# Attention scores in pairs of heads: QK matmuls ordered by head instead of by key tile

## The chip, the cores and the metric

One Trainium2 chip, all 8 cores, the same program on each with its own input. Cores 2b and 2b+1 share batch element b of four; each computes 2048 of its 4096 rows and holds all 4096 for keys and values. The metric is the device time of the slowest core in microseconds (us). TensorE is PE in the profile, VectorE DVE, ScalarE ACT, GpSimd POOL.

## The reference

Layernorm, attention with 16 heads of 64, residual; then layernorm, a mixture of 8 experts with a shared expert, residual. The change lies in the attention alone:

```python
Q = circulant(x, wq_c, wq_b)      # K, V the same; circulant = a dense 1024x1024 product
attn_logits = jnp.einsum('bqhd,bkhd->bhqk', Q, K) * scale   # scale = 64 ** -0.5
attn_weights = jax.nn.softmax(attn_logits, axis=-1)
out_heads = jnp.einsum('bhqk,bkhd->bqhd', attn_weights, V)
out = circulant(out_merge, wo_c, wo_b)
```

## The kernel before

Every instruction goes through `Sched.op`, which appends it to a list of its engine; line 77 issues them later, in that order, so all rows of the profile carry L77 and groups are told apart by tiles. An engine's instructions are issued in the order of its list, and an instruction with `waits` holds up what stands behind it until the named semaphores have reached their counts.

The stages are: layernorm and transposes of 4096 rows (to about 230 us); attention (to about 2330 us); output projection, second layernorm, router; the feed-forward part in 20 units; the output.

Attention runs over 8 pairs of heads (`p`, line 386). The two heads of a pair lie on the two halves of the partitions: head 0 on rows 0 to 63 of `QTp` and `KTp`, head 1 on rows 64 to 127. Each pair has 4 chunks of 512 queries (`c`, line 422), and each chunk 16 groups of two key tiles of 128 (`gi`, line 424). A group does, in the order in which it is written down:

- four QK matmuls (lines 437 to 448), 64 rows deep, 128 keys x 512 queries each: two key tiles for each of the two heads, into `psS[0]` for head 0 and `psS[1]` for head 1 (two banks each). The first matmul of head 0 waits until the exp of the group before has read `psS[0]` (`wsa`), the first of head 1 the same for `psS[1]` (`wsb`). The last matmul of each head counts up `pQK`.
- four PV matmuls of the group before (`emit_pv`, line 403), two for each head, into `psO`; each pair waits for the exp that made its weights.
- two exps on ACT (lines 452 to 461), one for each head, 128 x 1024 from `psS` into one of three buffers of `PT`. The exp of head 0 waits for `pQK` at one less than its count after the group's last QK. Unit u = 2 x group + head also waits for the PV matmuls of unit u - 3, which read the same buffer of `PT`.
- projection jobs of the next pair (`ProjQ.drain_to`, line 465): 4 for q, 8 for k, 32 for v, in this order, dealt out evenly over the 64 groups; a q or k job is 8 matmuls of 128x512, a v job 8 of 128x128. The last pair has none.

At the end of a chunk the PVs of the last group are done, then the row sums are copied (`lscr`), spread by matmuls of ones into `psS[1]`, inverted on DVE (`invl`), multiplied in (`stg`), and the two heads are put together by two matmuls that work on rows 0 to 63 (`identB`, `shift64`), before the QKs of the next chunk.

These lines set what an exp waits for:

```python
ws = [("pQK", nqk_b - (1 if h == 0 else 0))]
if u >= 3:
    ws.append(("pPV", pv_at[u - 3]))
```

Of the kernel before, what the change touches and what calls it, by code (L numbers as in the profile page):

```python
# [83 lines left out]
def build_program(dbg=(), last_phase=6):  # L84
# [33 lines left out]
    with ExitStack() as ctx:  # L118
# [145 lines left out]
        with ExitStack() as c2:  # L264
# [121 lines left out]
            for p in range(NPAIR):  # L386
                bp = p % 2
                if p + 2 < NPAIR:
                    emit_wdma(p + 2)
                if p + 1 < NPAIR:  # L390
                    nq = ProjQ(p + 1, [("pQK", pair_end[p - 1]["pQK"]),
                                       ("pPV", pair_end[p - 1]["pPV"])]
                               if p > 0 else [])
                else:
                    nq = None

                exp_at = {}
                pv_at = {}
                recip_at = {}
                evac_at = {}  # L400
                pend = []

                def emit_pv(job):
                    u, cc_, pts, h = job
                    ws = [("aE", exp_at[u])]
                    if u % UPC <= 1:
                        ws.append(("vT", evac_at.get(cc_ - 1, S.n("vT"))
                                   if cc_ > 0 else S.n("vT")))
                    vsl = slice(65 * h, 65 * h + 65)
                    k0_, glen_ = groups[(u % UPC) // 2]  # L410
                    for i in range(glen_):
                        kt = k0_ + i
                        S.op("tensor", "matmul",
                             psO[0:65, 512 * h:512 * h + 512],
                             Vp[bp][:, kt, vsl],
                             PT[:, pts, i * 512:(i + 1) * 512],
                             start=(kt == 0), stop=(kt == 31),
                             waits=ws if i == 0 else (),
                             inc="pPV" if i == glen_ - 1 else None)
                    pv_at[u] = S.n("pPV")  # L420

                for c in range(NCH):
                    qsl = slice(c * 512, (c + 1) * 512)
                    for gi, (k0, glen) in enumerate(groups):
                        ua = c * UPC + 2 * gi
                        ub = ua + 1
                        wsa = []
                        wsb = []
                        if ua >= 2:
                            wsa.append(("aE", exp_at[ua - 2]))  # L430
                            wsb.append(("aE", exp_at[ub - 2]))
                        else:
                            wsa = [("vT", S.n("vT")), ("vP", proj_done[p])]
                            wsb = list(wsa)
                        if c > 0 and ua == c * UPC:
                            wsb.append(("vT", recip_at[c - 1]))
                        for i in range(glen):
                            kt = k0 + i
                            for h, slot, ws0 in ((0, 0, wsa), (1, 1, wsb)):
                                rowsl = slice(64 * h, 64 * (h + 1))  # L440
                                S.op("tensor", "matmul",
                                     psS[slot][:, i * 512:(i + 1) * 512],
                                     KTp[bp][rowsl, kt * 128:(kt + 1) * 128],
                                     QTp[bp][rowsl, qsl],
                                     start=True, stop=True,
                                     tile_position=(64 * h, 0),
                                     waits=ws0 if i == 0 else (),
                                     inc="pQK" if i == glen - 1 else None)
                        nqk_b = S.n("pQK")
                        while pend:  # L450
                            emit_pv(pend.pop(0))
                        for h, u in ((0, ua), (1, ub)):
# [3 lines that stand above are left out]
                            S.op("scalar", "activation",  # L456
                                 PT[:, u % 3, 0:glen * 512],
                                 psS[u % 2][:, 0:glen * 512],
                                 AF.Exp, bias=C_M12, scale=C_EIGHTH,
                                 waits=ws, inc="aE")  # L460
                            exp_at[u] = S.n("aE")
                        pend.append((ua, c, ua % 3, 0))
                        pend.append((ub, c, ub % 3, 1))
                        if nq is not None:
                            nq.drain_to((2 * gi + 2) / UPC / NCH + c / NCH)
                    while pend:
                        emit_pv(pend.pop(0))
                    S.op("vector", "tensor_copy", lscr[64:65, 0, :],
                         psO[64:65, 0:512],
                         waits=[("pPV", None), ("pT", None)], inc="vT")  # L470
                    S.op("vector", "tensor_copy", lscr[64:65, 1, :],
                         psO[64:65, 512:1024], inc="vT")
                    S.op("tensor", "matmul", psS[1][0:64, 0:512],
                         onescolF[64:65, 0:64], lscr[64:65, 0, :],
                         start=True, stop=True,
                         waits=[("vT", None), ("aE", None)], inc="pT")
                    S.op("tensor", "matmul", psS[1][0:64, 512:1024],
                         onescolF[64:65, 0:64], lscr[64:65, 1, :],
                         start=True, stop=True, inc="pT")
                    S.op("vector", "reciprocal",  # L480
                         invl[0:64, :, :].rearrange("p a b -> p (a b)"),
                         psS[1][0:64, 0:1024],
                         waits=[("pT", None)], inc="vT")
                    recip_at[c] = S.n("vT")
                    S.op("vector", "tensor_tensor", stg[0:64, 0, :],
                         psO[0:64, 0:512], invl[0:64, 0, :], ALU.mult,
                         waits=[("vT", None), ("pT", None)], inc="vT")
                    S.op("vector", "tensor_tensor", stg[0:64, 1, :],
                         psO[0:64, 512:1024], invl[0:64, 1, :], ALU.mult,
                         inc="vT")  # L490
                    S.op("tensor", "matmul", psO[:, 0:512], identB[0:64, 0:128],
                         stg[0:64, 0, :], start=True, stop=False,
                         waits=[("vT", None)])
                    S.op("tensor", "matmul", psO[:, 0:512], shift64[0:64, 0:128],
                         stg[0:64, 1, :], start=False, stop=True, inc="pT")
                    S.op("vector", "tensor_scalar", outT[:, p, qsl], psO[:, 0:512],
                         biasT[:, 2 * NDT + p:2 * NDT + p + 1], None, ALU.add,
                         waits=[("pT", None)], inc="vT")
                    evac_at[c] = S.n("vT")
                if nq is not None:  # L500
                    nq.finish()
                pair_end[p] = {"pQK": S.n("pQK"), "pPV": S.n("pPV"),
                               "vT": S.n("vT")}

                if p == 0:
                    if "qt" in dbga:
                        S.op("gpsimd", "dma_start", out=dbga["qt"], in_=QTp[0][:],
                             waits=[("vP", proj_done[0])], inc="dbg90", inck=16)
                    if "kt" in dbga:
                        S.op("gpsimd", "dma_start", out=dbga["kt"], in_=KTp[0][:],  # L510
                             waits=[("vP", proj_done[0])], inc="dbg91", inck=16)
                    if "vt" in dbga:
                        S.op("gpsimd", "dma_start", out=dbga["vt"],
                             in_=Vp[0][:].rearrange("p a b -> p (a b)"),
                             waits=[("vP", proj_done[0])], inc="dbg92", inck=16)
# [478 lines left out]
```

How the kernel before makes its waits and increments, by code:

```python
            def runner(e, lst=lst):  # L72
                for meth, args, kw, ws, ih in lst:
                    for h, v in ws:
                        if v > 0:
                            e.wait_ge(h, v)
                    ins = getattr(e, meth)(*args, **kw)
                    if ih is not None:
                        ins.then_inc(*ih)
```

## Time and profile before

| | us |
|---|---|
| two timed runs | 5250.03, 5609.47 (median 5429.75) |
| profiled execution | 5131.93 |
| its span, slowest core (core 2) | 5130.4 |
| spans of the 8 cores | 5106.4 to 5130.4 |
| PE busy, share of the span | 3955.7, 77% |
| DVE busy | 1627.0, 32% |
| ACT busy | 1535.2, 30% |

The profile is of one execution and shows its slowest core. A busy time is the union of an engine's instructions; the idle time of a group is what the engine stood still just before instructions of that group, put down to what ended it. PEclk is the share of TensorE's 2.4 GHz that was granted: 1.00 is 2.4 GHz, 0.50 is 1.2 GHz, and what lies between is a mix of the two over a stretch.

### The profile page before, as it was taken

The page shows a single profiled execution, that of the slowest core. Times are in us where ns is not written, and L with a number is a line of the kernel's source. Part 1 is how long each engine was busy: PE and PEld are TensorE (multiplying, and loading weights), DVE is VectorE, ACT ScalarE, POOL GpSimd, SP SyncE. Part 2 cuts the span into 40 slices and gives each one's busy share as a digit, 9 for nine tenths or more (in the row PEclk, how much of TensorE's full clock was granted, in tenths as well). Part 3 has the DMA queues.
Part 4 walks back from the last instruction along what each step waited for, and adds up shares of the span by engine and source line. Part 5 has one row for each costly group of instructions (what it writes and reads, how often), then busy time and mean ns, then how long its engine had stood idle before and what let it go on. Part 6 is the DMA issues. An engine that isn't in the chain of part 4 may idle for free.

```text
span 5130.4 us, 58302 instructions; the slowest of 8 cores (5106.4 to 5130.4 us)
## 1 busy us (share of the span) xinstructions
PE 3955.7 (77%) x18399; PEld 1656.2 (32%) x18656; DVE 1627.0 (32%) x2454; ACT 1535.2 (30%) x1630; POOL 86.8 (2%) x107
## 2 busy tenths in 40 slices
PE   1566666666767676774359999999999999999996
PEld 0322222222222222111224444444444443444443
DVE  4322222222222122112344333333333434333344
ACT  3155555555555555551201111111111010111110
POOL 0100000000000000000000000000000000000000
PEclk9988888888888888666679999999999999999997
DMA  6300000000000000002142121212121213132103
GB/s 218 64 1 7 1 7 1 7 1 7 1 7 1 1 1 1 0 1 82 60 74 38 32 38 31 38 31 38 32 38 31 38 31 48 22 62 39 31 5 132
DMA packets 100824, 165.79 MB, mean 32 GB/s; under 512 B 28080, under 2 KB 69056, under 8 KB 100544
## 3 DMA queue, kind: packets, MB, share of 16 engines
q0 software_dynamic: 83072, 94.93, 12.2%
q1 hardware_dynamic: 17472, 67.11, 3.8%
q8 instruction: 177, 2.90, 0.2%
q14 instruction: 103, 0.84, 0.1%
HBM read 240.17 MB, written 16.78 MB: 50 GB/s over the span
## 4 chain that ended last, share of the span: by engine, by line
PE 69%; DVE 10%; ACT 10%; issue 8%; DMA 2%; DVEq 0%; ACTq 0%; POOL 0%; SPq 0%; POOLq 0%
PE psGU L77 30%; PE psD L77 15%; PE psS L77 9%; ACT PT L77 9%; PE psO L77 8%; DVE invl L77 4%; PE psP L77 4%; PE psT L77 1%; PE psC L77 1%; DMA xst<-xf 1%; DVE lscr L77 1%; DVE stg L77 1%; DVE us_sb L77 1%; DMA co_sb<-co 1%; DVE xnst L77 1%
## 5 line engine op out<-in xcount | busy, mean ns | idle before, releaser
L77 ACT ACTIVATE PT<-psS,consts 128x1024 bf16<-128x1024 f32 x1024 | 1182.2, 1199 | 1065.7 <-PE psS L77 1058.9
L77 ACT ACTIVATE gs_sb<-psGU 128x512 bf16<-128x512 f32 x440 | 262.7, 597 | 2143.4 <-PE psGU L77 2071.8
L77 PE MATMUL psD<-prod,wdh 128*128 128x512 bf16 x3449 | 778.9, 380 | 81.5 <-DVE prod L77 76.4
L77 PE MATMUL psGU<-xn2T,wgh 128*128 128x512 bf16 x3450 | 837.2, 383 | 4.2 <-issue 0.7
L77 PE MATMUL psGU<-xn2T,wuh 128*128 128x512 bf16 x3449 | 829.4, 380 | 3.9 <-issue 0.2
L77 PE MATMUL psS<-QTp,KTp 64*128 64x512 bf16 x2048 | 513.4, 421 | 308.3 <-ACT PT L77 296.8
L77 PE MATMUL psO<-PT,Vp 128*65 128x512 bf16 x2048 | 589.3, 411 | 26.4 <-ACT PT L77 26.4
L77 DVE TENSOR_TENSOR yacc<-yacc,psD 128x512 f32<-128x512 f32 x608 | 418.4, 688 | 371.2 <-PE psD L77 363.7
L77 PEld LDWEIGHTS psD<-prod,wdh 128*128 128x128 bf16 x3520 | 321.7, 97 | 538.7 <-issue 242.6
L77 DVE TENSOR_TENSOR us_sb<-psGU,ce_sb 128x512 bf16<-128x512 f32 x352 | 243.6, 692 | 793.4 <-PE psGU L77 793.4
L77 PEld LDWEIGHTS psGU<-xn2T,wgh 128*128 128x128 bf16 x3520 | 346.2, 99 | 423.8 <-issue 15.7
L77 PEld LDWEIGHTS psGU<-xn2T,wuh 128*128 128x128 bf16 x3520 | 346.1, 98 | 420.8 <-issue 9.9
L77 DVE CAST Vp<-psP 128x128 bf16<-128x128 f32 x256 | 75.4, 294 | 859.7 <-PE psP L77 859.7
L77 PEld LDWEIGHTS psO<-PT,Vp 128*65 128x65 bf16 x2048 | 193.8, 116 | 398.8 <-issue 309.7
L77 PEld LDWEIGHTS psS<-QTp,KTp 64*128 64x128 bf16 x2048 | 107.0, 96 | 600.2 <-issue 580.6
L77 DVE RECIPROCAL invl<-psS 64x1024 f32<-64x1024 f32 x32 | 209.6, 6550 | 116.1 <-PE psS L77 116.1
L77 PE MATMUL psO<-stg,identB 64*128 64x512 bf16 x32 | 18.6, 580 | 264.2 <-DVE stg L77 264.2
L77 DVE TENSOR_TENSOR prod<-gs_sb,us_sb 128x512 bf16<-128x512 bf16 x440 | 187.3, 426 | 84.6 <-DVE us_sb L77 83.5
L77 PE MATMUL psP<-cvp,xnT 128*128 128x128 bf16 x2048 | 166.8, 229 | 1.4 <-DVE KTp L77 0.6
L77 PEld LDWEIGHTS psP<-cvp,xnT 128*128 128x128 bf16 x2048 | 142.9, 103 | 67.4 <-issue 22.7
L77 PE MATMUL psS<-lscr,onescolF 1*64 1x512 f32 x128 | 104.6, 963 | 55.7 <-DVE lscr L77 55.7
L77 DVE COPY lscr<-psO 1x512 f32<-1x512 f32 x64 | 41.4, 684 | 322.3 <-PE psO L77 322.3
(105 smaller groups left out, 1215.5 us busy)
## 6 DMA issues: line engine op xcount, KB each, us to landing
xst<-xf SPq DMA_DIRECT2D x16, 2048.0 KB, 9.1
wgh<-wg POOLq DMA_DIRECT2D x8, 1536.0 KB, 15.0
wuh<-wu POOLq DMA_DIRECT2D x8, 1536.0 KB, 23.6
wdh<-wd POOLq DMA_DIRECT2D x8, 1536.0 KB, 30.2
wgh<-wg POOLq DMA_DIRECT2D x8, 1280.0 KB, 13.0
wuh<-wu POOLq DMA_DIRECT2D x8, 1280.0 KB, 19.4
wdh<-wd POOLq DMA_DIRECT2D x8, 1280.0 KB, 24.8
xo<-xf SPq DMA_DIRECT2D x4, 2048.0 KB, 10.8
```

The lines of the kernel that those rows point to most:

```text
L77: ins = getattr(e, meth)(*args, **kw)
```

## The change

The two loops around the QK matmul change places. Before, they are issued as head 0 tile 0, head 1 tile 0, head 0 tile 1, head 1 tile 1. After, both tiles of head 0 are issued and then both of head 1. Waits, counters, operands and everything else stay as they are.

```diff
-                        for i in range(glen):
-                            kt = k0 + i
-                            for h, slot, ws0 in ((0, 0, wsa), (1, 1, wsb)):
-                                rowsl = slice(64 * h, 64 * (h + 1))
+                        for h, slot, ws0 in ((0, 0, wsa), (1, 1, wsb)):
+                            rowsl = slice(64 * h, 64 * (h + 1))
+                            for i in range(glen):
+                                kt = k0 + i
                                 S.op("tensor", "matmul",
                                      psS[slot][:, i * 512:(i + 1) * 512],
                                      KTp[bp][rowsl, kt * 128:(kt + 1) * 128],
```

## Rows read from the trace of the kernel before

**Rows 1.** The page, first part: busy us (share of span) xinstructions.

```profile
span 5130.4 us, 58302 instructions; the slowest of 8 cores (5106.4 to 5130.4 us)
PE 3955.7 (77%) x18399; PEld 1656.2 (32%) x18656; DVE 1627.0 (32%) x2454; ACT 1535.2 (30%) x1630; POOL 86.8 (2%) x107
```

**Rows 2.** Windows: attention, and all behind it. Columns as the second line says.

```profile
core 2: us, PE busy (x) PEld busy (x) DVE busy (x) ACT busy (x) POOL busy (x), PEclk, DMA share, GB/s
228.00:2330.00 2102.00, 1446.51 (x6786) 525.65 (x6818) 443.64 (x507) 1182.20 (x1024) 15.79 (x18) 0.83 0.03 3
2330.00:5130.00 2800.00, 2442.01 (x11078) 1085.22 (x11298) 1085.09 (x1814) 314.27 (x539) 53.77 (x63) 0.94 0.24 44
```

**Rows 3.** Page, instruction groups: busy, mean ns | idle before, by releaser; last, waits.

```profile
L77 ACT ACTIVATE PT<-psS,consts 128x1024 bf16<-128x1024 f32 x1024 | 1182.2, 1199 | 1065.7 <-PE psS L77 1058.9
L77 PE MATMUL psS<-QTp,KTp 64*128 64x512 bf16 x2048 | 513.4, 421 | 308.3 <-ACT PT L77 296.8
...
PE psS L77 <- ACT PT L77: 296.8, 500, 1.5
```

**Rows 4.** Timeline, warm groups: start, duration, engine, xcount, idle before; last: narrow windows.

```profile
1092.65 2.30 ACT L77 ACTIVATE PT<-psS,consts 128x1024 bf16<-128x1024 f32 x2 [0.69 <-PE psS L77]
1093.29 0.65 PEld L77 LDWEIGHTS psP<-cvp,xnT 128*128 128x128 bf16 x8
1093.51 0.61 PE L77 MATMUL psP<-cvp,xnT 128*128 128x128 bf16 x8
1094.05 0.39 PE L77 MATMUL psS<-QTp,KTp 64*128 64x512 bf16 x1
...
1095.09 0.59 PE L77 MATMUL psS<-QTp,KTp 64*128 64x512 bf16 x3 [0.65 <-ACT PT L77]
...
1095.63 2.30 ACT L77 ACTIVATE PT<-psS,consts 128x1024 bf16<-128x1024 f32 x2 [0.69 <-PE psS L77]
...
1096.98 0.37 PE L77 MATMUL psS<-QTp,KTp 64*128 64x512 bf16 x1 [0.32 <-ACT PT L77]
...
1098.08 0.59 PE L77 MATMUL psS<-QTp,KTp 64*128 64x512 bf16 x3 [0.72 <-ACT PT L77]
...
1098.62 1.20 ACT L77 ACTIVATE PT<-psS,consts 128x1024 bf16<-128x1024 f32 x1 [0.69 <-PE psS L77]
...
1093.75 1.20 ACT L77 ACTIVATE PT<-psS,consts 128x1024 bf16<-128x1024 f32 x1
...
1095.30 0.37 PE L77 MATMUL psS<-QTp,KTp 64*128 64x512 bf16 x1
...
1095.61 1.05 PE L77 MATMUL psO<-PT,Vp 128*65 128x512 bf16 x4
...
1095.85 0.38 PE L77 MATMUL psO<-PT,Vp 128*65 128x512 bf16 x1
```

**Rows 5.** Timeline, groups with a k projection.

```profile
1053.33 0.61 PE L77 MATMUL psS<-QTp,KTp 64*128 64x512 bf16 x4
...
1053.87 1.05 PE L77 MATMUL psO<-PT,Vp 128*65 128x512 bf16 x4
...
1056.58 0.61 PE L77 MATMUL psS<-QTp,KTp 64*128 64x512 bf16 x4
```

**Rows 6.** Timeline, last pair, low clock; the last three from narrow windows.

```profile
2141.76 2.54 ACT L77 ACTIVATE PT<-psS,consts 128x1024 bf16<-128x1024 f32 x2 [0.91 <-PE psS L77]
...
2141.94 1.91 PE L77 MATMUL psO<-PT,Vp 128*65 128x512 bf16 x4
...
2145.21 2.54 ACT L77 ACTIVATE PT<-psS,consts 128x1024 bf16<-128x1024 f32 x2 [0.91 <-PE psS L77]
...
2141.38 0.63 PE L77 MATMUL psS<-QTp,KTp 64*128 64x512 bf16 x1
...
2142.37 0.63 PE L77 MATMUL psO<-PT,Vp 128*65 128x512 bf16 x1
...
2143.10 1.20 ACT L77 ACTIVATE PT<-psS,consts 128x1024 bf16<-128x1024 f32 x1
```

**Rows 7.** Windows by chunk, columns as in rows 2: first exp to start of the last.

```profile
1017.90:1068.10 50.20, 44.50 (x205) 16.41 (x208) 8.26 (x11) 35.56 (x31) 0.00 (x0) 0.97 0.00 1
1085.70:1132.60 46.90, 35.76 (x207) 14.87 (x206) 3.69 (x11) 35.55 (x31) 0.00 (x0) 0.97 0.00 1
1149.90:1197.40 47.50, 35.92 (x208) 15.15 (x206) 3.24 (x11) 35.66 (x31) 0.00 (x0) 0.93 0.00 1
2064.90:2111.60 46.70, 31.41 (x121) 8.99 (x120) 0.00 (x0) 35.72 (x32) 0.00 (x0) 0.93 0.00 1
2128.20:2181.00 52.80, 50.14 (x119) 11.79 (x120) 0.00 (x0) 37.19 (x31) 0.00 (x0) 0.50 0.00 0
2199.50:2248.20 48.70, 37.84 (x120) 9.97 (x120) 0.00 (x0) 36.23 (x32) 0.00 (x0) 0.77 0.00 0
2264.90:2317.80 52.90, 50.23 (x119) 11.79 (x120) 0.00 (x0) 37.12 (x32) 0.00 (x0) 0.50 0.00 0
...
301.50:348.00 46.50, 35.33 (x207) 14.82 (x206) 3.70 (x11) 35.57 (x32) 0.00 (x0) 0.98 0.00 1
```

**Rows 8.** Timeline, the start of a chunk.

```profile
1148.23 0.58 PE L77 MATMUL psS<-QTp,KTp 64*128 64x512 bf16 x1
1148.26 0.63 PE L77 MATMUL psO<-stg,shift 64*128 64x512 bf16 x1
```

## The prediction

> **What bounds the kernel now.** I read the page first, then stretches of the span, then single groups in the timeline. The page says that PE is busy 77% of the span and ACT 30% [rows 1]. Two stretches make up the span: attention, 2102 us, in which every QK, exp and PV of the kernel lies, and all that comes after it, 2800 us [rows 2]. The change touches only the first. The instruction groups show what is odd there: ACT works 1182 us on exps and stands idle 1066 us ahead of them, nearly all of it for the QK products in psS, while PE in turn waits 297 us for exps before it can write psS [rows 3]. Each waits for the other, so neither its busy time sets the pace; a loop does.
>
> The timeline of three key groups shows the loop [rows 4]. I call the two QK matmuls of head 0 A0 and A1, those of head 1 B0 and B1. From one first exp to the next it is 1095.63 - 1092.65 = 2.98 us, then 1098.62 - 1095.63 = 2.99, once with a v projection in it and once without. A0 goes out alone (1094.05, 1096.98), as soon as its half of psS is free. Then PE stands still 0.65 to 0.72 us, until expB has ended; then the other three QKs run, and 0.54 us after they began expA starts. So A1, which needs nothing from head 1, sits in PE's queue behind B0, which waits for expB. ACT pays for it: idle 0.69 us in each group. The period is 1.10 (expA to expB, 1092.65 to 1093.75) + 1.34 (expB to B0, 1093.75 to 1095.09) + 0.54 (B0 to expA) = 2.98.
>
> This holds for the groups with v projections and for those with none. With a q or k projection (8 matmuls of 512 columns) PE itself is full: the four QKs come out in one train of 0.61 us, and QK to QK takes 1056.58 - 1053.33 = 3.25 us [rows 5]. At the lower granted clock a group without projection takes 2145.21 - 2141.76 = 3.45 us [rows 6].
>
> How many of each: a pair of heads has 4 chunks of 16 groups. The jobs are dealt out evenly, so q and k fill chunk 0 and v the other three, for seven pairs; the eighth has none. A chunk from first expA to the start of the last expB takes 46.5 to 47.5 us in the v chunks (I looked at five), 50.2 in a q/k chunk, and 46.7 to 52.9 in the last pair, whose clock is 0.93, 0.50, 0.77, 0.50 [rows 7]. 46.9 - 1.1 = 45.8 is one slow interval of 4.0 and 14 of 2.99; 47.5 - 1.1 = 46.4 is two slow intervals of 3.4 and 3.8 and 13 of 2.99. So there are 7 x (14 + 13 + 13) = 280 warm groups of 2.99 us. In the last pair 196.7 us fit about 21 groups of 2.99 and 33 of 3.45.
>
> **The change, part by part.** No instruction is added or removed: 2048 QKs, as many weight loads, the same waits. Only B0 and A1 change places, and B0's wait now stands behind A1.
>
> *What goes.* A1 no longer waits for expB. In a warm group A0 starts at expA + 1.35 (1096.98 - 1095.63), A1 0.22 later, and its product is ready 0.53 us after it, at expA + 2.10. ACT is then still at expB (from 1.10 to 2.30). The old 0.69 us of idle goes.
>
> *What is late next.* Not ACT's own work. PT has three buffers, so expB of group g also waits for the first PV pair of group g-1 (pv_at[u - 3]). That pair stands in PE's queue behind B0 and B1 of group g, and B0 waits for expB of g-1. This closes a new loop, expB - B0 - B1 - PV - PV - expB. Its links from rows 4: expB to B0 1.34; B0 to B1 0.21 (1095.30); B1 to the first PV 0.31 (1095.61); to the second 0.24 (1095.85). The last link, second PV to expB, is not seen warm, since there it doesn't bind, but it is seen at the low clock: 2142.37 to 2143.10 = 0.73 us, and just there expB comes 1.34 us after expA instead of 1.10 [rows 6]: the wait is real. Two ways to carry it to the warm clock: the record is shorter by 0.63 - 0.38, giving 0.48; or the streaming of 512 columns is shorter (PV to PV 0.43 against 0.22), giving 0.52. I take 0.52. Sum: 1.34 + 0.21 + 0.31 + 0.24 + 0.52 = **2.62 us**, lower end 2.58. PE's own train has room in it: B0 to fourth PV 1.19, eight v matmuls and the step to A0 0.76 (1093.29 to 1094.05), A0 to A1 0.22, together 2.17. Saved per warm group: 2.99 - 2.62 = 0.37; 280 x 0.37 = **-104 us**.
>
> *Row halves.* The two heads use different halves of the array's rows. Four QKs take 0.61 us where four PVs take 1.05 [rows 5]: A and B run side by side. Queued as A0 A1 B0 B1, do they still? At a chunk's start, a QK matmul begins at 1148.23, ahead of the shift matmul at 1148.26 that stands before it in the queue [rows 8]. The shift works on rows 0 to 63, so that QK is B0 on rows 64 to 127, running ahead of A. The halves therefore keep their own order once nothing waits, and in the q/k groups I take the cost as 0. If B0 could only start together with A1, it would be one pass of 0.22 us more in 84 q/k groups (18 us) and 0.43 in 21 cold chunk starts (9 us); that is the bound from the other side. In the v and empty groups B0 has to wait for expB anyway, and the loss of concurrency costs only idle time of PE, already in the sum. The Trainium skill, "TensorE: Matmul & The Clock Gate", Part 3, has matmuls strictly first in, first out, which would give those 27 us and a sum of 5027. The order at 1148.23 disagrees, so the row decides.
>
> *At the low clock.* The same loop gives 1.34 + 0.43 + 0.56 (2141.38 to 2141.94) + 0.43 + 0.73 = 3.49 against 3.45. So the cold groups lose 0.04; with the cold starts of the v chunks +1 us.
>
> *The last pair.* It depends on the clock. If it stays cold as often as now: 21 x -0.37 + 33 x 0.04 = -6 us. If it warms up after three groups in each chunk: 4 x (3 x 3.49 + 12 x 2.62) = 168 against 196.7, -29 us. Now, cold, PE streams 7 passes of 0.43 in 3.45 us (87%) and the clock mostly stays low; cold v groups stream with no gap and reach the high level after two groups every time I looked (slow intervals of 3.4 and 3.8, then 2.99). After, A and B no longer share a pass: 8 x 0.43 in 3.49, 98%. That is nearer to the second case, so I take -29 and keep -6 for the range. "TensorE: Matmul & The Clock Gate", section "Why this matters for your kernels" in the Trainium skill, advises a continuously busy engine for the high level; it points the same way.
>
> *Chunk ends.* From the last expB to the next chunk's first expA nothing changes: two PVs, the sums, the 6.55 us reciprocal, the stg matmuls. The same projection jobs lie there. 0.
>
> **Sum.** The profiled execution took 5131.9 us for a span of 5130.4. 5131.9 - 104 + 1 - 29 = **5000 us**. The two runs shown before (5250.0 and 5609.5, median 5429.8) lie above it; the forecast is for an execution like the profiled one, and carries over as the ratio 0.974.
>
> **Rivals.**
> Main theory with the last pair's clock as now: 5131.9 - 104 + 1 - 6 = 5023, -2.1%.
> *ACT becomes the bound*: the PT wait doesn't bite when warm, and the next links decide: two exps of 1.10 give 2.21 us, 280 x 0.78 = 218 less, 4885. Against it stand the cold rows, in which the PT wait sets expB.
> *Weight loads come out of hiding*: two QKs in a row on the same rows can't load the second's weights during the first. Then B0 to B1 would be a whole matmul and load, 0.37 + 0.09 = 0.46 instead of 0.21, the loop 2.87, 280 x 0.12 = 34 less: 5098. Against it, B0 to B1 is already 0.21 with only A1 on the other rows between them.
> *Slower: the v chunks stay at the low clock.* Splitting the shared passes fills a cold v group: B0 to fourth PV 0.43 + 0.56 + 1.28, eight v matmuls at 0.11, the step 0.2, two QKs 0.86, about 4.1 us; with the empty ones at 3.5, 3.9 on average, 0.9 above now. All 280 cold would be +255, with -6 for the last pair 5381. Each cold group costs 0.9 and forfeits 0.37, so the sign turns at about 80 of 280. For it: the last pair does stay cold. Against it: PE has fewer gaps than now in every group.
> *Nothing happens*: expA keeps waiting for both heads. Its wait is the count reached with A1's increment, one short of B1's, before and after; little speaks for it.
>
> **Chances and range.** Main theory, last pair warm (5000): 0.45. Main, clock as now (5023): 0.25. Weight loads (5098): 0.10. Nothing (5132): 0.05. ACT bound (4885): 0.07. Low clock (over 5235): 0.08. The range takes the first three; downward it takes 2.58 as the loop's lower end (280 x 0.04 = 11 less) and a last pair that is warm from its first group (4 x 15 x 2.62 = 157, 11 less again), 4978, rounded to 4980; upward it ends at 5100. The 2% that a measurement can tell from no change is 103 us, below 5029. Faster: 0.45 + 0.07 + half of the 5023 case = 0.65. Within: the rest of it, 0.10 and 0.05 = 0.27. Slower: 0.08.
>
> **What would show it.** In v chunks, expA to expA 2.62 us, with expB 1.5 us after expA and released by PV; ACT's idle time ahead of the exps falls from 1066 to about 930 us, and part of it turns into waits for psO. A0 and A1 stand as two matmuls ahead of PE's wait, B0 and B1 behind. q/k groups stay at 3.25; 3.46 would mean that the halves don't run apart. v chunks take 41 to 42 us. I'd be wrong if the groups come out at 2.2 or 2.9, or if the v chunks show a clock well below 0.9.

## The result, and the profile after

The changed kernel takes 4994.9 us in the median of all its runs, the kernel before 5144.7 in the runs beside it. The ratio is 0.9722, with a 95% interval of 0.9682 to 0.9762: 2.8% faster. (In some executions of nearly every kernel here the cores of one die or both run at a lower clock for a part of the time; the ratios, and the times from here on, leave them out, and traces are read on cores that were not affected.) The forecast was 5000 us and a ratio of 0.974.

The profiled execution took 5029.6 us, with a span of 5028.1. It is 35 us above the median for one reason: behind attention this core and its neighbour, core 3, got a clock of 0.81 for about 250 us. Attention, where the change lies, is not touched by that on this core. Its page, first part, and the instruction groups that answer to [rows 3]:

```profile
span 5028.1 us, 58302 instructions; the slowest of 8 cores (4975.0 to 5028.1 us)
...
PE 4056.5 (81%) x18399; PEld 1677.0 (33%) x18656; DVE 1627.0 (32%) x2454; ACT 1541.6 (31%) x1630; POOL 86.8 (2%) x107
...
L77 ACT ACTIVATE PT<-psS,consts 128x1024 bf16<-128x1024 f32 x1024 | 1188.6, 1202 | 919.5 <-PE psS L77 846.1
...
L77 PE MATMUL psS<-QTp,KTp 64*128 64x512 bf16 x2048 | 601.3, 426 | 115.9 <-ACT PT L77 99.4
```

ACT does the same exps in nearly the same time and stands idle 920 us ahead of them instead of 1066. PE waits 99 us for exps instead of 297, and is busy longer with the same 2048 QKs (601 us against 513), because the two heads no longer share passes in most groups. Neither of the two busy times explains the gain.

Windows by chunk, as in [rows 7] (us, busy us of PE, PEld, DVE, ACT, POOL, PEclk, DMA share, GB/s): the q/k chunk and two v chunks of the fourth pair, the four of the last pair, then the 0.81 stretch:

```profile
959.60:1010.10 50.50, 45.60 (x205) 16.62 (x208) 8.26 (x11) 35.61 (x32) 0.00 (x0) 0.97 0.00 1
...
1027.40:1068.90 41.50, 38.47 (x207) 15.11 (x206) 3.69 (x11) 35.81 (x32) 0.00 (x0) 0.96 0.00 1
1084.70:1127.00 42.30, 39.15 (x208) 15.50 (x206) 3.24 (x11) 35.97 (x32) 0.00 (x0) 0.91 0.00 1
...
1929.00:1981.80 52.80, 51.50 (x120) 12.06 (x120) 0.00 (x0) 37.20 (x31) 0.00 (x0) 0.50 0.00 0
1998.40:2041.70 43.30, 37.00 (x120) 9.82 (x120) 0.00 (x0) 36.07 (x31) 0.00 (x0) 0.82 0.00 1
2057.90:2108.60 50.70, 48.28 (x120) 11.53 (x121) 0.00 (x0) 36.94 (x31) 0.00 (x0) 0.56 0.00 0
2125.50:2178.30 52.80, 51.40 (x119) 12.09 (x120) 0.00 (x0) 37.18 (x31) 0.00 (x0) 0.50 0.00 0
...
4710.00:4980.00 270.00, 252.76 (x963) 105.25 (x980) 93.99 (x148) 23.42 (x40) 0.57 (x1) 0.80 0.13 28
```

The same chunks took 50.2, 46.9 and 47.5 us. The last pair still spends most of its time at the low clock. I added up the trace of core 2 by kind of stretch. A chunk counts from the start of its first expB to that of its last, a chunk end from there to the next chunk's first expA:

| | before | after | difference | forecast |
|---|---|---|---|---|
| 21 v chunks | 963.6 | 854.6 | -109.0 | -103 |
| 7 q/k chunks | 345.6 | 345.7 | +0.1 | 0 |
| last pair | 196.6 | 195.3 | -1.3 | -29 |
| 31 chunk ends | 542.5 | 513.8 | -28.7 | 0 |
| behind attention | 2812.6 | 2849.7 | +37.1 (0.81 clock) | 0 |

The rest of the span changed by less than 1 us. On the cores of the other die, what lies behind attention takes 2808 to 2814 us, against 2805 to 2812 before. So the total came out right from four terms of which two were wrong, by amounts that nearly cancel: that part is luck.

The timeline of v groups in the changed kernel, and two narrow windows (the second PV, and B0 alone):

```profile
1045.61 2.30 ACT L77 ACTIVATE PT<-psS,consts 128x1024 bf16<-128x1024 f32 x2
...
1046.96 0.59 PE L77 MATMUL psS<-QTp,KTp 64*128 64x512 bf16 x2 [0.48 <-ACT PT L77]
...
1047.47 1.05 PE L77 MATMUL psO<-PT,Vp 128*65 128x512 bf16 x4
...
1048.19 1.20 ACT L77 ACTIVATE PT<-psS,consts 128x1024 bf16<-128x1024 f32 x1 [0.29 <-PE psO L77]
1048.36 0.61 PE L77 MATMUL psP<-cvp,xnT 128*128 128x128 bf16 x8
...
1049.66 2.32 ACT L77 ACTIVATE PT<-psS,consts 128x1024 bf16<-128x1024 f32 x2 [0.27 <-PE psS L77]
1050.06 1.05 PE L77 MATMUL psO<-PT,Vp 128*65 128x512 bf16 x4
...
1047.72 0.38 PE L77 MATMUL psO<-PT,Vp 128*65 128x512 bf16 x1
...
1049.54 0.37 PE L77 MATMUL psS<-QTp,KTp 64*128 64x512 bf16 x1
```

The exp at 1048.19 is an expB, and it waits for psO: the PV matmuls that free its PT buffer. The list of waits shows how often that happens, first before, then after (us in total, times, longest):

```profile
ACT PT L77 <- PE psO L77: 0.2, 1, 0.2
...
ACT PT L77 <- PE psO L77: 72.9, 207, 0.9
```

The new loop is there. From the B matmuls at 1046.96 to the next at 1049.54 it is 2.58 us, and PV to PV 1050.06 - 1047.47 = 2.59.

### The profile page after: what moved, and what is told of

Same layout as the page of the kernel before. It is cut to its first block, busy times and chain, and to the rows that moved or that the text cites. A ratio compares the mean times of both kernels' runs of the same rounds, so it can differ in the third digit from the quotient of the medians.

```text
span 5028.1 us, 58302 instructions; the slowest of 8 cores (4975.0 to 5028.1 us)
## 1 busy us (share of the span) xinstructions
PE 4056.5 (81%) x18399; PEld 1677.0 (33%) x18656; DVE 1627.0 (32%) x2454; ACT 1541.6 (31%) x1630; POOL 86.8 (2%) x107
## 4 chain that ended last, share of the span: by engine, by line
PE 76%; DVE 10%; ACT 6%; issue 5%; DMA 2%; DVEq 0%; ACTq 0%; POOL 0%; SPq 0%; POOLq 0%
PE psGU L77 31%; PE psD L77 15%; PE psS L77 11%; PE psO L77 10%; PE psP L77 6%; ACT PT L77 5%; DVE invl L77 4%; PE psT L77 1%; PE psC L77 1%; DMA xst<-xf 1%; DVE lscr L77 1%; DVE stg L77 1%; DVE us_sb L77 1%; DMA out<-obuf 1%; DVE xnst L77 1%
## 5 line engine op out<-in xcount | busy, mean ns | idle before, releaser
L77 PE MATMUL psD<-prod,wdh 128*128 128x512 bf16 x3449 | 791.6, 385 | 81.7 <-DVE prod L77 76.4
L77 PE MATMUL psGU<-xn2T,wgh 128*128 128x512 bf16 x3450 | 852.3, 388 | 4.5 <-issue 0.7
L77 PE MATMUL psGU<-xn2T,wuh 128*128 128x512 bf16 x3449 | 844.5, 386 | 4.1 <-issue 0.2
L77 PE MATMUL psS<-QTp,KTp 64*128 64x512 bf16 x2048 | 601.3, 426 | 115.9 <-ACT PT L77 99.4
L77 PE MATMUL psT<-identB,xnst 128*128 128x128 bf16 x256 | 32.3, 305 | 141.0 <-DVE xnst L77 141.0
```

Source lines behind the costliest of these rows:

```text
L77: ins = getattr(e, meth)(*args, **kw)
```

## Experiments

### Which loop sets the new period: a fourth PT buffer

```diff
-            PT = cc(nc.sbuf_tensor("PT", [128, 3, 1024], BF16))
+            PT = cc(nc.sbuf_tensor("PT", [128, 4, 1024], BF16))
...
-                            if u >= 3:
-                                ws.append(("pPV", pv_at[u - 3]))
+                            if u >= 4:
+                                ws.append(("pPV", pv_at[u - 4]))
```

(and u % 4 where u % 3 stood.) On the changed kernel:

> The changed kernel with four PT buffers instead of three, so that an exp waits for the PV matmuls of unit u - 4, which stand ahead of the B matmuls in PE's queue. Theory (after the change the loop expB - B0 - B1 - PV - PV - expB through the PT buffer sets the period of 2.59 us): it is broken, and the next one decides, from B0 over the four PVs to A0 and A1 of the next group, its two exps, and back to B0 after two groups: 1.50 + 0.22 + 0.54 + 1.10 + 1.34 = 4.70 us for two groups without a job, 0.45 more for each v job that it meets. v chunks at 2.45 to 2.55 a group on average, the sum over the 21 v chunks from 855 down to about 825 us, cold groups of the last pair from 3.45 to about 3.23; in all 30 to 40 us under the changed kernel's 4995, near 4960. Rival (the loop runs through psS, the buffer doesn't bind): v chunks stay at 855 us, 4995. Rival (ACT alone binds once PT is free): 2.21 a group, 4885.

It took 4936 us (one execution), against 4995. v chunks add up to 826 us. Core 4, the first chunk of the last pair, exps in sequence:

```profile
1930.11 4.49 ACT L77 ACTIVATE PT<-psS,consts 128x1024 bf16<-128x1024 f32 x4 [0.21 <-PE psS L77]
1934.81 4.49 ACT L77 ACTIVATE PT<-psS,consts 128x1024 bf16<-128x1024 f32 x4 [0.21 <-PE psS L77]
```

Two groups in 4.70 us, the sum named beforehand, and ACT idle 0.21 us in them. Neither rival survives: the buffer did bind, and ACT alone doesn't. In the v chunks the next loop lies close behind: from the fourth interval of each chunk on, 252 in all, a group takes 2.50 us on average instead of 2.59. The time fell by 59 us rather than 30 to 40, because the last pair also left the low clock (its chunk from 1914.4 to 1952.2, 37.8 us, ran at 0.92), which I had not counted on. Chunk ends grew again, to 525 to 530 us.

The same buffer on the kernel before:

> The kernel before with four PT buffers, nothing else. Theory: warm groups don't change (2.99 us), since there PV is done 0.35 us before expB could start; only groups at the low clock, where expB came 1.34 us after expA, gain 0.24 us each, some 33 in the last pair and 21 at chunk starts: -8 to -13 us, near 5122. Rival (the PT buffer already cost time before the change, and its wait was merely hidden by how the trace names releasers): v chunks fall by more than 20 us from 964.

5115.3 us in the median, ratio 0.9965 (0.9945 to 0.9984). v chunks stay at 965, so before the change the buffer cost nothing in a warm group. The gain lies in the last pair, core 2:

```profile
2054.00:2100.40 46.40, 31.84 (x121) 9.14 (x120) 0.00 (x0) 35.62 (x32) 0.00 (x0) 0.91 0.00 1
2116.20:2162.90 46.70, 31.36 (x120) 9.10 (x120) 0.00 (x0) 35.65 (x32) 0.00 (x0) 0.92 0.00 1
```

These are the first two chunks of the pair, which took 46.7 and 52.8 us before. In the second, 6 us is more than 0.24 us a group: the clock rose, here and in the last pair of all eight cores, with no matmul added. The sum over the pair fell by 15 us on core 2. The size is near the forecast of 8 to 13, but the way is partly another.

### Where the gain lies, and the row halves

```diff
-                        for i in range(glen):
+                        order = [(i, h) for h in (0, 1) for i in range(glen)]
+                        if c > 0 or p == NPAIR - 1:
+                            order = [(i, h) for i in range(glen) for h in (0, 1)]
+                        for i, h in order:
...
```

That is the new order in the q/k chunks alone; its counterpart has `if c == 0 and p < NPAIR - 1`, the new order everywhere else.

> The new order in chunk 0 of the seven pairs that carry q and k projections, the old order everywhere else. Theory (matmuls on different row halves keep their own order, so A0 A1 B0 B1 takes two passes like A0 B0 A1 B1 once nothing waits): the q/k chunks' sum stays at 345 us, the time within 3 us of 5132. Rival (strict order, three passes): 0.22 us more in 84 groups, q/k chunks at about 360 us, 5150.

> The counterpart of qk_chunks_only: the new order in the 21 v chunks and the last pair, the old one in the seven q/k chunks. Theory (the whole gain lies where B waits for its exp and PE has room): v chunks at 855 us, q/k chunks at 345, the time like the changed kernel's, 4995 within 8 us. Rival (part of the gain of the full change comes through the q/k chunks, by the clock with which the chunk behind them begins): above 5005.

The first gave 5130.8 us, ratio 0.9991 (0.9970 to 1.0012), with q/k chunks at 344 to 348 us. The second gave 4995.9, ratio 0.9742 (0.9714 to 0.9770), with v chunks at 854 to 855. So the q/k chunks cost nothing, and everything is gained in the rest. How A0 A1 B0 B1 costs no third pass can be seen in a q/k group of the changed kernel:

```profile
1004.93 0.61 PE L77 MATMUL psS<-QTp,KTp 64*128 64x512 bf16 x4
1005.47 1.05 PE L77 MATMUL psO<-PT,Vp 128*65 128x512 bf16 x4
...
1008.18 0.61 PE L77 MATMUL psS<-QTp,KTp 64*128 64x512 bf16 x4
```

The four QKs take 0.61 us as in [rows 5], and the group 3.25 us. Two narrow windows show that they start in pairs:

```profile
1004.93 0.39 PE L77 MATMUL psS<-QTp,KTp 64*128 64x512 bf16 x2
...
1005.16 0.38 PE L77 MATMUL psS<-QTp,KTp 64*128 64x512 bf16 x2
```

The trace doesn't name the heads. But A0 and A1 use the same rows, and two matmuls on the same rows, B0 and B1 in [rows 4], start 0.21 us apart. So the pair at 1004.93 is A0 and B0: B0 has overtaken A1.

### The last pair: is it the amount of work?

```diff
+                        if nq is None:
+                            for dt in range(NDT):
+                                S.op("tensor", "matmul", psP[gi % 2][:, 0:128],
+                                     xnT[:, dt, gi * 128:(gi + 1) * 128],
+                                     cvp[bp][:, dt, :],
...
```

> The changed kernel, and in every group of the last pair 8 more matmuls of 128x128 into a PSUM bank that nobody reads, where a v job would stand. Nothing of the result changes. Theory (the last pair stays at the low clock because it gives PE less work than the other pairs, whatever the order): its clock rises after two or three groups of each chunk, its groups go from 3.45 to 2.59 us, its chunks from 51.7 to about 42 us, together about 25 to 35 us less, near 4965, although PE does more. Rival (the clock in the last pair hangs on something else): the groups stay at the low clock and PE is full, 4.1 us each, 25 us or more above 4995.

4964.5 and 4968.8 us, ratio 0.9675 (0.9634 to 0.9717): 26 to 30 us under the changed kernel, by adding 512 matmuls that nobody needs. Its interval overlaps that of the changed kernel, but the traces tell the two apart: the last pair takes 163 us on all eight cores, against 190 to 201 without the filling. Core 2:

```profile
1928.50:1970.20 41.70, 40.38 (x241) 17.71 (x241) 0.00 (x0) 35.94 (x31) 0.00 (x0) 0.92 0.00 1
1986.10:2028.00 41.90, 40.29 (x240) 17.47 (x238) 0.00 (x0) 35.91 (x31) 0.00 (x0) 0.92 0.00 1
```

All four chunks of all eight cores do this, where on core 2 three of four ran at 0.50 to 0.56 without the filling. The runs with four PT buffers got there too, without added work but with shorter groups: 3.21 us against 3.45 at the start of a chunk in the old order.

### The chunk ends: order or clock?

Many chunk ends of the changed kernel are about 1.5 us shorter. The timeline of one in the kernel before, behind the first v chunk of the fourth pair:

```profile
1136.26 3.37 PE L77 MATMUL psS<-lscr,onescolF 1*64 1x512 f32 x4 [1.72 <-DVE lscr L77]
...
1139.73 6.55 DVE L77 RECIPROCAL invl<-psS 64x1024 f32<-64x1024 f32 x1 [3.72 <-PE psS L77]
```

And of the same one in the changed kernel:

```profile
1072.55 1.90 PE L77 MATMUL psS<-lscr,onescolF 1*64 1x512 f32 x4 [1.72 <-DVE lscr L77]
...
1074.55 6.55 DVE L77 RECIPROCAL invl<-psS 64x1024 f32<-64x1024 f32 x1 [2.25 <-PE psS L77]
```

The stall ahead is the same 1.72 us; the four fp32 matmul records (two matmuls in the program) take 3.37 us in the one and 1.90 in the other. Over all chunk ends of core 2 the time from their start to that of the reciprocal falls from 104.2 to 75.8 us, which is the whole gain of 28.7 to within 0.3. They took 2.34 to 3.64 us before; after, they take 1.90 behind 19 of the 21 v chunks, and still 2.08 to 3.64 behind the seven q/k chunks. The windows over just these stretches give the granted clock. Before, the stretch above and one of 3.64 us:

```profile
1136.20:1139.80 3.60, 3.37 (x4) 0.64 (x4) 0.07 (x1) 0.00 (x0) 0.00 (x0) 0.55 0.00 0
1071.70:1075.50 3.80, 3.64 (x4) 0.73 (x4) 0.00 (x0) 0.00 (x0) 0.00 (x0) 0.50 0.00 0
```

After:

```profile
1072.50:1074.60 2.10, 1.90 (x4) 0.45 (x4) 0.05 (x1) 0.00 (x0) 0.00 (x0) 1.00 0.00 0
```

To tell clock from order, the old order with six matmuls of no use in that stall:

```diff
+                    for m in range(6):
+                        S.op("tensor", "matmul", psP[nq.j % 2 if nq else 0][:],
+                             xnT[:, m % NDT, 0:128], xnT[:, m % NDT, 0:512],
...
```

> The kernel before, with only the 6 matmuls of 128x512 ahead of the matmuls of ones at every chunk's end. Theory (clock): the old order gets the short chunk ends too, 541 down to 515 or less over the 31 of them, near 5105. Rival (order): they stay at about 541, 5132.

5099.0 us, ratio 0.9917 (0.9890 to 0.9944); the 31 chunk ends fall from about 541 to 501.5 us, with v chunks at 961 to 963. A chunk end on core 7, with the filler ahead of it, and the granted clock over its fp32 matmuls:

```profile
1115.40 1.46 PE L77 MATMUL psP<-xnT 128*128 128x512 bf16 x6
...
1117.28 1.90 PE L77 MATMUL psS<-lscr,onescolF 1*64 1x512 f32 x4 [0.42 <-DVE lscr L77]
...
1117.20:1119.30 2.10, 1.90 (x4) 0.45 (x4) 0.02 (x1) 0.00 (x0) 0.00 (x0) 1.00 0.00 0
```

So the new order isn't needed for a short chunk end; the clock is enough. Then the filling on the changed kernel, with 30 more behind the matmuls of ones, under the reciprocal:

> The changed kernel, and at every chunk's end 6 matmuls of 128x512 into an unused PSUM bank ahead of the matmuls of ones and 30 behind them, while PE would wait for DVE; nothing of the result changes. Theory (the unforeseen 24 us between chunks are the clock's: the fp32 matmuls of ones take 2.0 us until the reciprocal starts at the high level and 3.7 at the low one, and so are the first two slow groups of a chunk): all chunk ends take the short form, from 513 to about 490 us or less over the 31 of them, and the chunks lose their slow start of 3.4 and 3.8 us against 2.59; together 50 to 90 us less, 4905 to 4945. Rival (chunk ends became shorter because the last groups' PVs end earlier in the new order, whatever the clock): chunk ends stay at 513, and 36 more matmuls cost up to 10 us.

4916.3 us, ratio 0.9562 (0.9529 to 0.9595). The chunk ends take 475 us instead of 513, the v chunks 822 to 834 instead of 855. The bigger part of the latter is the slow start of 3.4 and 3.8 us, which is gone from second and third v chunks; the first v chunk of a pair still begins with an interval of 4.0. Core 1, a chunk end and the chunk behind it:

```profile
1040.90:1055.90 15.00, 14.05 (x57) 5.23 (x56) 9.63 (x6) 1.22 (x3) 0.00 (x0) 0.89 0.00 0
1055.90:1096.00 40.10, 36.38 (x207) 14.51 (x204) 3.48 (x12) 35.74 (x31) 0.00 (x0) 1.00 0.00 1
```

40.1 us where the same chunk of the changed kernel takes 42.3.

### Moving the v jobs: a miss

On top of the fourth buffer, each v job between A1 and B0 of its group:

```diff
                         for h, slot, ws0 in ((0, 0, wsa), (1, 1, wsb)):
+                            if h == 1 and nq is not None and nq.j >= 12:
+                                nq.drain_to((2 * gi + 2) / UPC / NCH + c / NCH)
...
```

> The changed kernel with four PT buffers, and each v job issued between the two heads' QK matmuls of its group, where PE waits for expB, instead of behind the PVs. Theory (with four buffers the loop B0 - four PVs - A0 - A1 - expA - expB - B0 over two groups decides, and v jobs lengthen it by 0.45 us where it meets them): the v jobs leave the loop, v chunks come to 4.70 / 2 = 2.35 us a group like the last pair, their sum from 826 with four buffers alone to about 770 us, the time about 55 us under the 4936 of the fast execution with four buffers, near 4880. Rival (PE's own queue, with its switches between kinds of matmul, is the bound in v chunks): the sum stays within 10 us of 826.

Core 2 spans 4937 us, with v chunks at 821: next to no gain beside 826, and the fastest run took 4945.6 us, no less than the 4936 without the move. The rival's number holds. PE around a v group:

```profile
1043.36 1.05 PE L77 MATMUL psO<-PT,Vp 128*65 128x512 bf16 x4
1044.35 0.60 PE L77 MATMUL psS<-QTp,KTp 64*128 64x512 bf16 x2
1044.88 0.62 PE L77 MATMUL psP<-cvp,xnT 128*128 128x128 bf16 x8
1045.43 0.60 PE L77 MATMUL psS<-QTp,KTp 64*128 64x512 bf16 x2
1045.96 1.05 PE L77 MATMUL psO<-PT,Vp 128*65 128x512 bf16 x4
```

From train to train there is no gap left, and the group takes 2.60 us. The job between the heads adds two more switches between 64-row and 128-row matmuls, and A and B can't share a pass: it left one loop and filled PE. That isn't all of it. From the fourth interval of a chunk on, the groups average 2.44 us against 2.50 without the move, 15 us less over the 21 v chunks. The third intervals take back 11, and the first exps of a chunk, which this sum leaves out, another 12: from the first expA to the first expB, the 32 chunks together take 47.2 us instead of 35.3.

### Versions that beat both

> The new order, four PT buffers, v jobs between the heads, and the 36 matmuls at chunk ends. Theory: the gains add, since they lie in different loops: about 4880 less 50 to 90, 4790 to 4830. Rival (more work on PE brings the clock down in attention or behind it): above 4880.

> The new order, four PT buffers and the 36 matmuls at chunk ends, the v jobs in their old place behind the PVs. It tells what of the combined kernel comes from the place of the v jobs. Theory (with four buffers a v group holds PE for 2.60 us with the job between the heads, for about 2.5 on average with the job behind the PVs, so that moving the jobs brings next to nothing): v chunks within 10 us of the combined kernel's 800, 4850 to 4880. Rival (the combined kernel needs the move): v chunks at 820 or more, 4885 and up.

> The new order with three PT buffers, the 36 matmuls at chunk ends, and the 8 unused matmuls in each group of the last pair. Theory (work, and with it the clock, is what both places lacked; the two add): edge_fill's 4916 less what its last pair still stands above 4 x 39 us, 15 to 30 us, near 4890.

The combined kernel took 4856.6 and 4868.0 us, which is above the 4790 to 4830 that its theory named: the moved jobs bring next to nothing, as above, so that term is missing. Without the move, the fourth buffer and the filled chunk ends give 4856.1 us in the median, ratio 0.9468 (0.9447 to 0.9490): 2.8% under the changed kernel, as fast as the combined one and simpler. Some chunks still start slowly, such as the last one here. Core 2, a v chunk, the end behind it, and the next v chunk:

```profile
987.70:1026.30 38.60, 36.15 (x207) 14.75 (x206) 3.93 (x12) 35.59 (x32) 0.00 (x0) 1.00 0.00 1
1026.30:1041.30 15.00, 12.57 (x58) 5.00 (x57) 9.63 (x6) 1.22 (x3) 0.00 (x0) 1.00 0.00 0
1041.30:1081.30 40.00, 36.00 (x205) 14.86 (x203) 3.48 (x12) 34.99 (x32) 0.00 (x0) 0.96 0.00 1
```

The last kernel, three buffers with both fillings, took 4885.7 us (one execution), near the 4890 named.

## Why the prediction was right, and where it was wrong

**A1 no longer waits for expB.** Right. A0 and A1 stand together ahead of PE's wait, and the idle time of ACT falls by 146 us in the page.

**The PT buffer takes over.** Right. The exp at 1048.19 waits for psO, the period is 2.59 us, and a fourth buffer brings it to 2.35 where there are no jobs. In such a group the loop costs 0.24 us: the gain is 0.40 us with it and 0.64 without. In the v chunks it costs 0.09, because PE's queue with the v jobs is nearly as slow. The rival "ACT becomes the bound" would have given 0.78. Of the links only the last one was mis-sized: second PV to expB takes 1048.19 - 1047.72 = 0.47 us, the lower of the two ways to carry it over (0.48), not the 0.52 that I took. That is 280 x 0.035 = 10 us more than forecast, near -113 with the +1. On core 2 only 275 intervals are of this kind, not 280, and the 40 others take 143 us where 37 took 133 before; so the v chunks came to -109.

**Row halves run apart.** Right: q/k chunks +0.1 us, and 5130.8 us with the change in them alone. The Trainium skill, "TensorE: Matmul & The Clock Gate", Part 3, has matmuls start and end strictly in program order; for matmuls on different row halves [rows 8] and the starts in pairs (1004.93 and 1005.16) speak against it, and the measurement decides. A wait is another matter: behind an instruction that waits for a semaphore both halves stop. Before, A1 stood 1.04 us behind A0 (1094.05 and 1095.09), though all that it waited for was its turn behind B0; that is where the gain in the groups comes from.

**The last pair.** Wrong, and the step that failed is "that is nearer to the second case, so I take -29". I read the clock off the share of time in which PE streams: 87% before, 98% after. The changed kernel streams 51.50 us of 52.80 in one of its four chunks and 51.40 in another, and both stay at 0.50. With 8 small matmuls more in each group, and 97% busy too, the clock rises; with a fourth buffer in the old order it rises while PE is busy 67% of the chunk (31.36 of 46.70 us). So the busy share didn't tell the cases apart. The filling shows that more work in the same groups is enough, and the fourth buffer that shorter groups are. What exactly the chip weighs stays open. The case that came about is the second one of the prediction, with the clock as now: 5023 us, with a chance of 0.25, and the 5000 was met because the chunk ends gave what the last pair didn't. Two smaller things: a cold group takes 3.45 us as before, not 3.49; and the pair had 22 groups at 2.99 and 36 at 3.45 before, where the prediction counted 21 and 33 of its 60, which changes its sum by less than 1 us.

**Chunk ends.** The step "from the last expB to the next chunk's first expA nothing changes" was right for the work and wrong for the time. The instructions are the same, but the fp32 matmuls in them take 1.90 us at the high level and up to 3.64 at the low one. -29 us on core 2, -23 to -25 on the cores of the other die. That the clock alone can shorten a chunk end is shown (six useless matmuls do it in the old order). Why the high level lasts through these matmuls behind most v chunks of the new order, and not behind the q/k chunks or in the old order, isn't.

**Rivals.** The ACT-bound case would have needed more than a fourth buffer (2.35 us a group with one, not 2.21). Weight loads stay hidden: from B0 at 1049.54 over B1 to the first PV at 1050.06 it is 0.52 us, the 0.21 and 0.31 of [rows 4]. The v chunks didn't fall to the low clock: 0.91 to 0.96.

## What to carry to other kernels

When two chains share one engine's queue, ask for each instruction what the one in front of it waits for: an order that alternates between chains ties each to the other's waits, even where the hardware would run them side by side. Then find the next loop before predicting the gain, by following the buffers with their counts through the same queue; here a limit of three buffers that had cost nothing took back 0.24 of 0.64 us in a group without jobs. And price short fp32 or small matmuls after a stall at both clock levels, since the stretch in front of them decides which one they get.

## What the runs showed of the hardware

Useless matmuls in PE's idle time made the kernel faster three times: 26 to 30 us in the last pair, about 37 us with 6 in each chunk end of the old order (5099.0 against 5136.4 in the runs beside it), 79 us with 36 in each of the new order. Two fp32 matmuls of one row and 512 columns, four records in the trace, took 3.64 us at the low level and 1.90 at the high one, more than four bf16 QK matmuls (0.61 us as a train). A third level appears beside the two: behind attention, two cores of a die stood at 0.81 for some 250 us, and what lies behind attention took 37 and 38 us longer on them than before. The Trainium skill, "TensorE: Matmul & The Clock Gate", Part 1, names such a limit of 13/16 for dies with three or more busy cores. The 0.80 of the window 4710 to 4980 agrees with its size. The condition doesn't agree: in the profiled execution of the kernel before, with all eight cores busy, each core was granted 0.99 from 2700 to 5000 us.
